# Reordering the head normalisation in the first two batches of a two-layer transformer kernel

## What is computed

```python
proj = x @ w_qkv                                   # per batch: 256 tokens
q, k, v = jnp.split(proj, 3, axis=-1)              # 16 heads of width 16
q = apply_rope(q, cos, sin); k = apply_rope(k, cos, sin)
q = layernorm(q, ln_scale, ln_bias)                # over the 16 columns of a head
k = layernorm(k, ln_scale, ln_bias)
a = jnp.einsum('bhnd,bhmd->bhnm', q, k) ** 4
a = jnp.tril(a)
out = jnp.einsum('bhnm,bhmd->bhnd', a / jnp.sum(a, -1, keepdims=True), v)
x = _layernorm(x + out @ w_out)
```

## Time and profile before

| | us |
|---|---|
| median of 3 runs | 876.03 (875.99 to 877.25) |
| the profiled execution | 876.34 |
| its span | 874.6 |
| TensorE busy in the span | 806.8 (92%) |
| VectorE busy | 667.3 (76%) |
| ScalarE busy | 579.4 (66%) |
| GpSimd busy | 422.2 (48%) |

### The profile page before, as it was taken

The page is one execution under the profiler, slowest core; times in us unless marked ns, Lnnn a source line. Parts: engine busy times, 40 slices in busy tenths (PEclk is TensorE's granted clock), DMA queues, the critical chain, the costliest instruction groups (busy, mean ns, idle before and its releaser), DMA issues.

```text
span 874.6 us, 20901 instructions
## 1 busy us (share of the span) xinstructions
PE 806.8 (92%) x7097; PEld 677.9 (78%) x7097; DVE 667.3 (76%) x2136; ACT 579.4 (66%) x1232; POOL 422.2 (48%) x725
## 2 busy tenths in 40 slices
PE   4876999999999999899999999999998999999994
PEld 3554778888888899667777777777766988999984
DVE  5987889888896555778898888979886463487657
ACT  2777868687787533677878777777766233366646
POOL 0353223233253311576767667676765357355423
PEclk9899999999999999999999999999999899999998
DMA  7111220201001010111010211201013112345444
GB/s 218 35 40 43 80 86 12 87 14 37 26 1 49 25 38 25 43 34 31 22 55 23 63 42 37 66 22 43 23 59 120 37 64 95 92 129 134 128 161 170
DMA packets 55017, 54.86 MB, mean 63 GB/s; under 512 B 18209, under 2 KB 49185, under 8 KB 54914
## 3 DMA queue, kind: packets, MB, share of 16 engines
q1 hardware_dynamic: 51506, 44.18, 17.1%
q0 software_dynamic: 3408, 9.34, 3.1%
HBM read 32.85 MB, written 20.65 MB: 61 GB/s over the span
## 4 chain that ended last, share of the span: by engine, by line
PE 68%; DVE 15%; ACT 9%; issue 6%; POOL 1%; DMA 1%; DVEq 0%; ACTq 0%; SPq 0%; POOLq 0%
PE ps L448 13%; PE ps L449 12%; PE ps L450 12%; PE ps L992 10%; PE ps L1003 5%; PE ps L684 3%; PE ps L731 2%; DVE G L2182 2%; PE ps L771 2%; PE ps L976 2%; DVE wu_rows L2182 2%; ACT G L1596 1%; PE ps L1249 1%; PE ps L753 1%; PE ps L1213 1%
## 5 line engine op out<-in xcount | busy, mean ns | idle before, releaser
L2568 POOL TENSOR_SCALAR_AFFINE_SELECT G<-G 128x256 f32<-128x256 f32 x128 | 75.9, 617 | 150.1 <-ACT G L1422 149.9
L1596 ACT ACTIVATE G<-ps 128x512 f32<-128x512 f32 x184 | 102.7, 602 | 39.9 <-PE ps L992 38.3
L448 PE MATMUL ps<-WU 128*128 128x256 f32 x384 | 116.3, 303 | 11.4 <-DVE WU L1977 6.5
L2616 POOL TENSOR_SCALAR G<-G,small 128x256 f32<-128x256 f32 x214 | 99.8, 483 | 51.6 <-DVE small L2182 49.9
L2182 DVE CUSTOM_DVE_ANT_0 G<-ps,nb 128x256 f32<-128x256 f32 x296 | 108.3, 420 | 10.6 <-PE ps L731 9.4
L449 PE MATMUL ps<-WU 128*128 128x256 f32 x384 | 108.3, 282 | 0.0
L450 PE MATMUL ps<-WU 128*128 128x256 f32 x384 | 108.3, 282 | 0.0
L2616 POOL TENSOR_SCALAR wu_rows<-wu_rows,small 128x256 f32<-128x256 f32 x154 | 71.7, 482 | 38.7 <-DVE small L2182 37.7
L448 PEld LDWEIGHTS ps<-WU 128*128 128x128 f32 x384 | 72.8, 190 | 18.0 <-DVE WU L1977 7.3
L992 PE MATMUL ps<-ident,G 128*128 128x128 f32 x592 | 83.5, 278 | 3.0 <-ACT G L1596 2.9
L2182 DVE CUSTOM_DVE_ANT_0 wu_rows<-ps,nb 128x256 f32<-128x256 f32 x216 | 79.5, 420 | 7.4 <-PE ps L731 6.5
(11 more groups left out here) (267 smaller groups left out, 2356.2 us busy)
## 6 DMA issues: line engine op xcount, KB each, us to landing
xs<-G SPq DMA_DIRECT2D x8, 645.0 KB, 6.6
G<-xs SPq DMA_DIRECT2D x39, 128.0 KB
G<-x SPq DMA_DIRECT2D x17, 256.0 KB, 3.1
G<-in_x SPq DMA_DIRECT2D x16, 256.0 KB, 2.8
wu_rows<-yy SPq DMA_DIRECT2D x8, 512.0 KB, 7.0
x<-G SPq DMA_DIRECT2D x15, 256.0 KB, 2.2
wu_rows<-in_wu SPq DMA_DIRECT2D x8, 384.0 KB, 4.9
wraw<-in_wu SPq DMA_DIRECT2D x16, 128.0 KB, 2.2
```

Source lines behind the costliest of these rows:

```text
L448: pe.matmul(o, lh, rh, start=start, stop=False, skip_group_check=True)
L1596: act.activation(probT(n), halves(2 + n % 2), ACT.Exp).then_inc(probT_taken, 1)
L2568: m = pool.affine_select(out=u, in_=u, compare_op=ALU.is_ge, fill=0.0, base=0, pattern=[[0, 2], [1, P]], channel_multiplier=-1)
L2616: m = pool.tensor_scalar(p, p, -1.0, mneg[:, k:k + 1], ALU.mult, ALU.add)
```

## The change

Three of the five engines get another order in batches 0 and 1; no step is added or taken out.

- TensorE, p = 4: `x_turn` of batch i + 2 stands ahead of the wait for `context` and of `heads(i, 3)`, not behind them.
- ScalarE, p = 4: `x_hi` and `deviation` stand ahead of `turned_heads(i, 3)`.
- VectorE: in p = 3 `variance` stands ahead of `context`; in p = 4 `normalised` stands ahead of `quartic` (the fourth power); `x_lo` of batch i + 2 stands behind both in batch 0, and behind `plus_bias` of p = 5 in batch 1.

```diff
@@ TensorE, dense(i, p) @@
                     if p == 4:
+                        if i < LAG1:
+                            pe.wait_ge(v_staged[0], i + 2)
+                            x_turn(0, i + 2)
                         if i:
                             pe.wait_ge(ctx_done[0], 2 * i)
                         heads(0, i, 3)
-                        if left > 1:
+                        if left > 1 and i >= LAG1:
                             pe.wait_ge(v_staged[0], i + 2)
                             x_turn(0, i + 2)
@@ ScalarE, narrow_slot(i, p) @@
                     if p == 4:
-                        turned_heads(i, 3)
                         x_hi(0, i + 2)
                         deviation(i + 1)
+                        turned_heads(i, 3)
@@ VectorE, narrow_slot(i, p) @@
                     if p == 3:
                         times_scale(i + 1)
+                        variance(i + 1)
                         if i:
                             for c in range(2):
                                 context(0, i - 1, c, D0)
-                        variance(i + 1)
                     if p == 4:
+                        normalised(i + 1)
                         quartic(i, p, not i)
-                        x_lo(0, i + 2)
-                        normalised(i + 1)
+                        if not i:
+                            x_lo(0, i + 2)
                     if p == 5:
                         if i:
                             context_lo(0, i - 1)
                         plus_bias(i + 1)
+                        if i:
+                            x_lo(0, i + 2)
```

## The result

The changed kernel takes 882.86 us (median of 8 executions, 878.56 to 885.64), the kernel before 876.75 beside it: a ratio of 1.0064, 95% interval 1.0039 to 1.0088. It is slower, by 6.1 us in the medians, where 2.4 were forecast. Its eight executions differ by 7 us, and most of what follows is about where these 7 us come from.

What follows compares the result with a forecast made beforehand. In batch 1 no engine was full; a chain of hand-overs set the pace. 0.45 (batch 0) + 0.65 (late project) + 1.3 (low clock) = +2.4 us on 876.03: 878.4, range 877.6 to 879.2, with rivals 875.6 to 880.3.

Steps and rivals of the forecast that it cites:

- Batch 0: First batch: VectorE waits 0.52 us for the deviation, and the batch hands over 0.45 us later (0.3 to 0.55).
- Batch 1 up to the bias: Reciprocal 1.9 us earlier, 0.8 of it lost waiting for `context_hi`, 0.9 to the fourth power; 0.2 left at the bias.
- Behind the bias: Batch 1: TensorE's project waits for the late `x_lo`, starting at 72.43 instead of 70.39; later heads move by 1.1 us.
- The waits' sum of 1.1: Batches 0 and 1: 0.45 handed over plus 0.65 for the late project, without any price for the clock.
- So a delay there stays: Behind the first gate matmul, to the end: TensorE's work has no load or store setting a date, so delay remains.
- the term of 1.3: Batch 1: 2.9 us idle brings one low clock stretch over project, mix and heads (2, 0), costing 1.3 us (1.1 to 1.7).
- rival 2: More clock falls, as over heads (1, 3) to `ct_turn`, hold up the bias; total +4 us, 880.0; chance 0.12.
- 878.7 on that basis: Whole kernel: time expected for a profiled execution, against 876.34 before the change.
- The trace agrees in the two falls, both behind idle time: TensorE's clock falls at 48.8 and 86.4, both behind idle stretches, taken to support the skill's rule.
- The range: Whole kernel: the forecast's own 877.6 to 879.2 us, widened by rivals to 875.6 to 880.3.
- Rival 4: Batch 2's idle time absorbs the 1.1 us delay, or an earlier low stretch disappears and repays it: 876.0; chance 0.10.

Runs made afterwards that it cites:

- fill_project: The changed kernel with 20 transposes that nobody reads on TensorE ahead of the project of batch 1 alone: 878.64 us, ratio 1.0015 to the kernel before.
- before_filled: The kernel before with unread transposes on TensorE ahead of five waits of batches 0 to 2 (4, 10, 10, 14, 22): 875.82 us, ratio 0.9985.
- again: The changed kernel once more, without an edit, for the spread of its runs and a second profile: 883.75 us, its profiled execution 883.22.
- after_filled: The changed kernel with unread transposes on TensorE ahead of four waits of batches 0 to 2 (14, 14, 20, 22): 876.91 us, ratio 0.9992 to the kernel before.
- before_fill_gate: The kernel before with 22 unread transposes on TensorE ahead of the first gate matmul alone: 875.71 us, ratio 0.9977.
- before_filled_start: The kernel before with five waits filled by unread transposes, and 34 more ahead of the queries of batch 1: 878.69 us, ratio 1.0006 to the kernel before.

## Why the prediction was wrong

- **Batch 0**: right. 0.52 of waiting and 0.45 handed over were forecast; the wait is 0.42, and the queries `qk(0, 2, 1)` start at 52.69, 0.68 late (0.49 without the 0.19 of the start) where 0.51 was forecast, released by VectorE's rope as said. The low stretch moved from 48.8 to 45.4, and nothing was won by it.
- **Batch 1 up to the bias**: right. Forecast: the reciprocal at 65.75 + 0.45 = 66.2, a wait of 0.8 for `context_hi`, the bias at 69.94 + 0.45 = 70.4. Measured: 66.34, 0.84, 70.59; 66.15 and 70.40 without the 0.19.
- **Behind the bias**: right. Project forecast at 72.43, found at 72.58 (72.39), released by `x_lo`. The waits' sum of 1.1 measured 1.32 (55.44 less 54.12), the price of the one low stretch over the project, 1.3, measured 1.43 (56.88 less the 55.45 of `fill_project`, whose profile has the same low stretch in batch 0).
- **"So a delay there stays"** and the sum of **one** low stretch, the term of 1.3: this is the step that failed. The prediction took the profile's low stretches of before (86.4, 683.7, 697.3) as they stood, and counted one more. They are not tied to an instruction: they come in some executions and not in others, even behind the same wait (1.96 us, above). With the project's wait filled, executions over 881 us went from 12 of 16 to none of 12 (on another chip). In four of six profiles of the changed kernel there were three to five more (of 3.4 us each, between 30 and 710 us) than in the first one: over the scores, the mix or `ct_turn` behind the heads (1, 3) (rival 2, given 0.12: 58.05 to 59.19 up to the gate), a double one at the gate (40.0 to 40.1 for 37.9), and in two of them 13.7 us for 6.8 at the router (42.4 for 39.2 to 40.0). The 6.1 us of the medians less the 1.32 of the waits leave 4.8 where the prediction had 1.3.
- **The near hit of the first profile is partly luck.** 2.4 us held for the two short executions (878.56 and 879.12 for 878.7 on that basis), but from another sum: 0.2 at the start and 2.7 up to the gate, less 1.1 and 0.3 behind it, and 0.7 more at the router, which the prediction did not have.
- **"The trace agrees in the two falls, both behind idle time"** passed over the falls at 683.7 and 697.3 of the same trace, which stand behind no wait of this kind (the router part, above).
- **The range** ended at 880.3. It went by one execution's clock, with rival 2 as the worst case, and no case in which low stretches add up. By the mean clock, 3 of 16 executions of the changed kernel were of the kind that was forecast (0.985 or more), 13 were not (0.977 or less).
- **Rival 4** (a low stretch that was there before pays it back) did occur in the first profile, 1.1 us behind the gate.
- The Trainium skill (TensorE: Matmul & The Clock Gate, "What's actually happening") was read with the right sign: the longer idle time does speak against the change. `fill_project` agrees, with 4 us for a wait filled.

Shown: the clock's part of the loss up to batch 2 follows TensorE's idle waits, since filling them takes it away with the order of all steps as it was, and leaves the 1.32 us of the waits. Argued only: that the router part (39.2 to 42.4) depends on how late the work arrives there. It was 42.4 in two long executions, 39.2 in two others, and 40.9 in before_filled; no run separates it. Open: what lengthens some executions of the kernel before at a mean clock of 0.983.

## What to carry to other kernels

Before moving a step behind another, list every wait that its result ends, on every engine. Here `x_lo` was moved behind the bias because the bias is on the chain, but it also held TensorE's next bank. And a wait of TensorE can cost twice: its length, and the clock of what follows. Where a wait of 2 us or more can't be removed, transposes that nobody reads, a little shorter than the wait, are worth a try: one such place made the kernel before 0.23% faster (0.09 to 0.36). Measure each place: a further one, in the wait at the start, gained nothing.

One profile is one draw. When the mean clock of single executions differs (0.985 and 0.972 here), the low stretches have to be counted over several profiles before any of them goes into a sum. And where executions differ at the same mean clock, look for a late transfer.

## What the runs showed of the hardware

- In four of six profiles of the changed kernel the clock fell behind TensorE's idle wait of 2.14 us ahead of the heads (1, 3), in `again` from 66.5 on; in two of these it fell once more behind the 2.63 to 2.65 ahead of the project, in the other two it stayed low over it. In the remaining two profiles it fell behind 2.88 us there but not behind the 2.14. Behind the 1.96 us of the kernel before it fell in one profile of two.
- At the router the clock fell from 2.4 to 1.2 GHz behind 3.63 us of matmuls of 18 columns, without a wait: TensorE was busy for 3.60 of the 3.60 us ahead.
- TensorE's work at 1.2 and at 2.4 GHz side by side: the heads (8 transposes) 1.97 and 1.09 us, the mix (16 matmuls) 1.51 and 0.86.
- The Trainium skill (TensorE: Matmul & The Clock Gate, "Why this matters for your kernels") advises to leave no long idle gaps between bursts of matmuls. The runs agree (`after_filled`: 876.91 for 883.75). They add that filling a gap with useless transposes cost nothing measurable up to the gate where the gap was longer than they are: `before_fill_gate` has 54.08 us from scores to gate, 54.18 without. `before_filled_start` lost 3 us, elsewhere and for a reason that is open.
